# One attention key step in two in split fp32r products, with two output banks and the weight split moved behind the attention

## What is computed

```
mod = silu(c) @ ada_w.T + ada_b                       # shift, scale, gate for attention and for the MLP
qkv = modulate(rmsnorm(x)) @ qkv_w.T + qkv_b           # q and k are rms-normed per head
attn = softmax(q k^T / 6);  o = attn v                 # B=2, H=16, N=2048, 36 wide
x = x + tanh(gate_msa) * (o @ proj_w.T + proj_b)
x = x + tanh(gate_mlp) * (gelu(modulate(rmsnorm(x)) @ fc1_w.T) @ fc2_w.T)
```

## Time and profile before

| what | us |
|---|---|
| median of 3 runs | 3037.22 (3037.14 to 3039.31) |
| the profiled execution | 3036.84, its span 3035.0 |
| TensorE matmuls busy | 2951.3 (97%) |
| ACT busy | 1574.1 (52%) |
| VectorE busy | 1208.0 (40%) |
| POOL busy | 204.6 (7%) |

### The profile page before, as it was taken

How to read it: one execution, slowest core, us unless ns; L and a number is a source line. 1 busy time by engine, 2 the same in 40 slices (tenths; PEclk the granted TensorE clock), 3 DMA queues, 4 the chain that set the end, 5 groups by cost and what they waited for, 6 DMA issues and landing times.

```text
span 3035.0 us, 36177 instructions
## 1 busy us (share of the span) xinstructions
PE 2951.3 (97%) x12968; PEld 1903.2 (63%) x12968; DVE 1208.0 (40%) x1540; ACT 1574.1 (52%) x1918; POOL 204.6 (7%) x126
## 2 busy tenths in 40 slices
PE   7999996999999999999999999999999999999998
PEld 7898993444444444444444444578888888888886
DVE  5887872333322322322322322434242442424242
ACT  3333323666666666666666666644343443434342
POOL 3232303520000000000000000000000000000000
PEclk7999997999999999999999999999999999999999
DMA  5454535232221222222222223131322222232121
GB/s 206 146 190 156 177 131 193 71 100 70 72 78 56 69 79 71 67 75 62 68 74 75 69 68 105 55 102 48 109 88 72 85 73 76 82 104 90 39 70 44
DMA packets 215540, 278.24 MB, mean 92 GB/s; under 512 B 15984, under 2 KB 125040, under 8 KB 214384
## 3 DMA queue, kind: packets, MB, share of 16 engines
q1 hardware_dynamic: 210160, 266.11, 27.7%
q10 hardware_dynamic: 5248, 10.49, 1.0%
HBM read 191.86 MB, written 84.67 MB: 91 GB/s over the span
## 4 chain that ended last, share of the span: by engine, by line
PE 80%; DVE 2%; DMA 1%; ACT 1%; SPq 0%; issue 0%; POOL 0%; DVEq 0%; POOLq 0%
PE ps L1257 23%; PE ps L1246 17%; PE ps L1307 14%; PE ps L1294 14%; PE ps L1256 7%; PE ps L1272 4%; ACT gated L1032 1%; DVE x L1164 0%; DMA vp<-v_scratch 0%; DVE rlb L1109 0%; DMA w_raw<-w 0%; DMA l_scratch<-osb 0%; DVE rlb L1103 0%; DVE w_lo L1158 0%; DVE x L1168 0%; DVE x L1170 0%
## 5 line engine op out<-in xcount | busy, mean ns | idle before, releaser
L985 ACT ACTIVATE prob<-ps 128x1024 f32<-128x1024 f32 x1084 | 979.3, 979 | 509.8 <-PE ps L1246 509.8
L1256 PE MATMUL ps<-prob,vp 128*64 128x512 f32 x2048 | 950.1, 601 | 2.7 <-DMA vp<-v_scratch 1.8
L1257 PE MATMUL ps<-prob,vp 128*37 128x512 f32 x2048 | 942.9, 598 | 0.0
L1246 PE MATMUL ps<-qT,kT 110*128 110x512 f32 x2048 | 564.4, 412 | 20.0 <-DMA qT<-m_scratch 18.7
L1246 PEld LDWEIGHTS ps<-qT,kT 110*128 110x128 f32 x2048 | 360.9, 189 | 346.0 <-ACT prob L985 193.5
L1257 PEld LDWEIGHTS ps<-prob,vp 128*37 128x37 f32 x2048 | 207.3, 114 | 389.2 <-issue 389.2
L1020 ACT ACTIVATE act<-ps,f1b_t 128x512 f32<-128x512 f32 x144 | 99.2, 689 | 509.1 <-PE ps L1294 509.1
L1097 DVE COPY osb<-ps 101x512 f32<-101x512 f32 x64 | 44.3, 692 | 751.8 <-PE ps L1257 748.6
L1256 PEld LDWEIGHTS ps<-prob,vp 128*64 128x64 f32 x2048 | 254.2, 136 | 119.7 <-issue 111.6
L1103 DVE RECIPROCAL rlb<-rlb 101x256 f32<-101x256 f32 x128 | 215.3, 1724 | 253.9 <-DMA rlb<-l_scratch 253.9
L1211 DVE TENSOR_TENSOR a_lo<-act,a_hi 128x512 fp32r<-128x512 f32 x144 | 99.6, 692 | 534.3 <-ACT a_hi L1022 534.3
(11 more groups left out here) (148 smaller groups left out, 2925.6 us busy)
## 6 DMA issues: line engine op xcount, KB each, us to landing
w_raw<-w SPq DMA_DIRECT2D x144, 320.0 KB, 2.9
qk_hi_scratch<-aw SPq DMA_DIRECT2D x32, 576.0 KB, 3.1
qk_lo_scratch<-aw SPq DMA_DIRECT2D x32, 576.0 KB, 4.4
kT<-qk_hi_scratch SPq DMA_DIRECT2D x128, 144.0 KB
qT<-qk_hi_scratch SPq DMA_DIRECT2D x128, 144.0 KB
v_scratch<-stv SPq DMA_DIRECT2D x32, 512.0 KB, 2.6
vp<-v_scratch SPq DMA_DIRECT2D x16, 1024.0 KB, 6.1
xb<-xT SPq DMA_DIRECT2D x8, 1280.0 KB, 9.9
```

The costliest lines, as they stand in the source:

```text
L985: act.activation(prob[:, slot, h0 * BLK:h1 * BLK], src, ACT.Exp).then_inc(exp_done, 1)
L1246: mm = pe.matmul(out, kT[r][:, h, kt * P:(kt + 1) * P], qT[:, c % 2, h], start=True, stop=True)
L1256: pe.matmul(O[0:64], vp[r][:, kt, 0:64], prob[:, j, 0:BLK], start=kt == 0, stop=kt == NT - 1)
L1257: pe.matmul(O[64:VW], vp[r][:, kt, 64:VW], prob[:, j, BLK:2 * BLK], start=kt == 0, stop=kt == NT - 1).then_inc(pv_mm, 1)
```

## The change

Attention is no longer a loop of hardware iterations but written out. The key steps 0 to 3 and 12 to 15 of a unit (SPLITS) are done as "split" steps: DVE makes `p_hi` (a cast, high_p) and `p_lo` (a subtraction, low_p) of the 128x1024 probabilities, and TensorE does four fp32r matmuls, for each head [v_hi | v_lo] (101 columns) times p_hi and times p_lo. Head 0 goes to bank OA and head 1 to bank OBK, where high and low land in partitions 0 to 63 and 64 to 100 (for head 1 the other way round). DVE splits the values once in a group (split_v). The steps 4 to 11 stay fp32 and are done in one block at the unit's end. The values of split steps 12 to 15 are done in the next unit, between its scores 2 and 6.

ACT now empties OBK (take_ob), DVE OA (take_oa); DVE adds the halves (combine: two copies and two additions). The sums are loaded spread over 128 partitions, inverted as 128x8 (invert_sums), stored, and loaded back broadcast; the rest of the unit's ending (finish_o) comes one unit later. The new buffers lie where the split `w2` was, so `w2` is loaded after the last value matmul, in four parts, and split by POOL during MLP block 0. `wp` is split by POOL in five pieces in the early units.

```diff
+RING = 3
+SPLITS = (0, 1, 2, 3, 12, 13, 14, 15)
+EARLY = NS // 2
+HIGHS = 6
...
+    LATE = (OS - W2) // (8 * D)
+    W2_FROM = (0, 2, 8, LATE)
...
         def spread_sums(u):
-                sp.wait_ge(o_evac, u + 1)
+                sp.wait_ge(o_comb, 2 * u + 2)
                 for h in range(2):
+                    sp.dma_start(lt[64 * h:64 * h + 64],
+                                 osb[64 * h + HD:64 * h + HD + 1].rearrange("a (p j) -> a p j", p=64)).then_inc(lt_ld, 16)
+                sp.wait_ge(l_rec, u + 1)
+                sp.dma_start(l_s.rearrange("h (p j) -> (h p) j", p=64), lt[:]).then_inc(l_st, 16)
+                sp.wait_ge(l_st, 16 * u + 16)
+                sp.dma_start(rlb[0:64], l_s[0].partition_broadcast(64)).then_inc(l_ld, 16)
+                sp.dma_start(rlb[64:VW], l_s[1].partition_broadcast(VW - 64)).then_inc(l_ld, 16)
...
+            for u in range(NU):
+                g, c = u // C, u % C
+                if u + 1 < NU:
+                    load_q(u + 1)
...
+                if u == LAST:
+                    sp.wait_ge(s_mm, NT * LAST)
+                    load_x(0)
+                if u > 1:
+                    store(u - 2)
+                if u == LAST:
+                    sp.wait_ge(o_dma, ODMA * (LAST - 2))
+                    load_o(0)
+                if u > 0:
+                    spread_sums(u - 1)
+                if u == LAST + 3:
+                    load_o(1)
+            sp.wait_ge(s_mm, NT * NU)
             load_w1(0)
             load_w1(1)
-            sp.wait_ge(pv_mm, NT * NU)
+            sp.wait_ge(fv_mm, NW * NU)
             load_x(1)
+            sp.wait_ge(rv_mm, NS * NU)
+            load_w2(0, 2)
+            load_w2(2, 8)
+            load_w2(8, LATE)
+            store(NU - 2)
             spread_sums(NU - 1)
-            store(NU - 1, PAIRS - 1, 1, C - 1)
             load_o(2)
...
+            pool.wait_ge(hlo_done, KC)
             for k in range(FC):
+                if k in W2_FROM:
+                    pool.wait_ge(w2_ld[W2_FROM.index(k)], 16)
```

ACT:

```diff
+            for u in range(NU):
+                for kt in range(NT):
+                    if NT * u + kt in PROJ_BEFORE:
+                        proj_gate(0, PROJ_BEFORE.index(NT * u + kt))
+                    if u > 0 and kt == 6:
+                        take_ob(u - 1)
+                    exps(u, kt)
+                if u == LAST + 2:
+                    for m in range(KC):
+                        act.wait_ge(x1_done, m + 1)
+                        act.activation(tmp[:, m], x1[0][:, m], ACT.Square).then_inc(sq_done, 1)
```

DVE (VectorE):

```diff
+            def combine(u):
+                dve.wait_ge(oa_evac, u + 1)
+                dve.wait_ge(ob_evac, u + 1)
                 wait(dve, o_dma, ODMA * u)
...
+            for u in range(NU):
+                if u > 1:
+                    finish_o(u - 2)
+                high_p(u, 0)
+                high_p(u, 1)
+                low_p(u, 0)
+                high_p(u, 2)
+                low_p(u, 1)
+                if u > 0:
+                    take_oa(u - 1)
+                high_p(u, 3)
+                low_p(u, 2)
+                low_p(u, 3)
+                if u > 0:
+                    combine(u - 1)
+                if u % C == 2 and u // C + 1 < NG:
+                    split_v(u // C + 1)
...
+                if u == LAST + 3:
+                    sum_squares(0)
+                high_p(u, 4)
+                high_p(u, 5)
+                low_p(u, 4)
+                high_p(u, 6)
+                low_p(u, 5)
+                if u > 0:
+                    invert_sums(u - 1)
+                high_p(u, 7)
+                low_p(u, 6)
+                low_p(u, 7)
...
+            reciprocal(0, 0)
+            reciprocal(0, 1)
+            finish_o(NU - 2)
+            take_oa(NU - 1)
+            for m in range(KC):
+                normed(0, m)
+            combine(NU - 1)
+            add_proj(1, 0)
+            add_proj(1, 1)
             for m in range(KC):
                 h_low(0, m)
+            invert_sums(NU - 1)
             split_w1(0)
```

TensorE:

```diff
+            for u in range(NU):
+                for kt in range(3):
+                    score(u, kt)
+                for j in range(EARLY):
+                    if u > 0:
+                        split_value(u - 1, EARLY + j)
+                    if j < 3:
+                        score(u, 3 + j)
...
+                for kt in range(6, 9):
+                    score(u, kt)
+                for j in range(EARLY):
+                    split_value(u, j)
+                    if j < 3:
+                        score(u, 9 + j)
...
+                for kt in range(12, NT):
+                    score(u, kt)
+                for kt in WHOLE:
+                    value(u, kt)
+            sum_rows(0)
+            proj(1, 0)
+            for j in range(EARLY, NS):
+                split_value(NU - 1, j)
+            for m in range(1, KC):
                 proj(1, m)
```

More of the change, by code:

```diff
@@ L608, in _, with place, ring_of_step, ring_of_proj @@
                 turn(NTILES - 1, 1)
[L611 to L619, removed]
+RING = 3
 C = NIT
 NU = B * PAIRS * C
+NG = B * PAIRS
 LAST = NU - C
 NB = B * NIT
[L626 to L651, removed]
+SPLITS = (0, 1, 2, 3, 12, 13, 14, 15)
+NS = len(SPLITS)
+EARLY = NS // 2
+WHOLE = range(EARLY, NT - EARLY)
+NW = len(WHOLE)
+HIGHS = 6
+PROJ_BEFORE = (NT * LAST + 12, NT * (LAST + 1) + 6, NT * (LAST + 1) + 12, NT * (LAST + 2) + 6, NT * (LAST + 2) + 12)
+def place(u):
+    return u // C // B, u // C % B, u % C
+def ring_of_step(n):
+    return n + sum(n >= b for b in PROJ_BEFORE)
+def ring_of_proj(m):
+    return PROJ_BEFORE[m] + m
+SUMS_ENTRY = NT * NU + KC
 def columns_of(i):
@@ L704, in main_phase @@
     here[0] = SQ
+    rb0 = at("rb0", [P, BLK], F32, here[0])
     sq0 = following("sq0", [P, 2, BLK], F32R)
@@ L893, in _ @@
             sp.wait_ge(kones, 1)
-            load_k(0, 0, 0)
-            load_q(0, 0, 0, 0)
+            load_k(0, 0)
+            load_q(0)
+            load_v(0)
             for c in range(1, C):
[L897 to L931, removed]
@@ L987, in proj_gate, with take_ob @@
+            def take_ob(u):
+                act.wait_ge(rv_mm, NS * (u + 1))
+                wait(act, o_comb, 2 * u)
+                act.activation(ob[:], OBK[0:VW], ACT.Copy).then_inc(ob_evac, 1)
             def proj_gate(i, m):
@@ L1249, in values, with ring_free @@
-            def values(u, r, kts, final):
-                for kt in kts:
-                    if kt == 0:
-                        wait(pe, o_evac, u)
-                    pe.wait_ge(exp_done, exps_before(u) + exp_index(kt, 1, final) + 1)
-                    j = kt % PSLOTS
-                    pe.matmul(O[0:64], vp[r][:, kt, 0:64], prob[:, j, 0:BLK], start=kt == 0, stop=kt == NT - 1)
-                    pe.matmul(O[64:VW], vp[r][:, kt, 64:VW], prob[:, j, BLK:2 * BLK], start=kt == 0,
-                              stop=kt == NT - 1).then_inc(pv_mm, 1)
+            def ring_free(entry):
+                before = entry - RING
+                for m in range(KC):
+                    if before == ring_of_proj(m):
+                        pe.wait_ge(pgate_done, m + 1)
+                        return
+                wait(pe, exp_done, before + 1 - sum(before > ring_of_proj(m) for m in range(KC)))
@@ new lines, in score @@
+            def score(u, kt):
+                it, r, c = place(u)
+                entry = ring_of_step(NT * u + kt)
+                if kt == 0:
+                    pe.wait_ge(q_ld[u % 2], QDMA * (u // 2 + 1))
+                if c == 0 and kt % TPB == 0:
+                    pe.wait_ge(k_ld[r][kt // TPB], KDMA * (it + 1))
+                ring_free(entry)
+                for h in range(2):
+                    mm = pe.matmul(ps[:, 2 * (entry % RING) + h, :], kT[r][:, h, kt * P:(kt + 1) * P], qT[:, u % 2, h],
+                                   start=True, stop=True)
+                mm.then_inc(s_mm, 1)
```

366 lines of the change are left out of this document (196 added, 170 removed).

## The result

| kernel | median us | range | runs |
|---|---|---|---|
| before | 3037.18 | 3035.46 to 3039.31 | 4 |
| changed | 3350.39 | 3346.11 to 3357.6 | 4 |

The changed kernel takes 1.1033 times as long, with a 95% interval of 1.101 to 1.1056: 313 us more, where I had forecast 3035 us and a range that ended at 3070. Its profiled span is 3351.6 us, against 3035.0.

A forecast was written before the change was run, and what follows sets the result against it. TensorE's own pace was taken to bound the attention, before and after the change. From 3037 us: attention 27 less, start 4 less, last group 5 more, transition to the MLP 24 more, giving 3035 us; range 3006 to 3070.

The forecast's parts named there:

- sums out and back: In each unit, inverted sums stored and loaded back broadcast, from invert_sums to finish_o: 3.8 us.
- the ring: In each attention unit, the loop of waits through DVE, the sums' transfers, TensorE and ACT: 22.1 us, shorter than 22.45.
- score 15's wait: In each unit, TensorE stands 0.57 us before score 15, which needs exponential 12.
- Rival 2: Slower: DVE is the bound in attention, 23.0 us a unit without instruction overlap, 3065 to 3070 us in all; chance 0.20.
- TensorE's work: In each attention unit, matmuls and changes between fp32r and fp32 sum to 21.8 us, about 1.0 below 22.87.
- rival 3: Far slower: in attention every change of stationary shape costs time, 185 us in 64 units, about 3220 us; chance 0.04.
- 0.3 us to spare: In each attention unit, the margin by which the loop of waits through DVE is shorter than TensorE's 22.45 us.
- Attention, 27 us less: Over 64 attention units, 22.45 us each in place of 22.87: 27 us less.
- DVE's durations: In each attention unit, 0.61 us for high_p and 1.13 for low_p with overlap; DVE's work 19.5 of 22.4 us.
- Start, 4 us less: From first matmul to first evacuation, 33 us before: 4 us less, between 0 and 8.
- Last group, 5 more: In the last attention group, 2.5 us waiting for load_o(0) and 2.5 for held-back exponentials: 5 us more.
- Attention to MLP, 24 more: Between attention and fc1, waits for load_o(1) and for the store behind w2: 24 us more, between 14 and 31.

The follow-up runs named there:

- e1: Changed kernel with the second load of the sums to 36 rows instead of 37; 3064.21 us, 1.009 times before.
- e10: Changed kernel with the second load of the sums over 64 rows instead of 37; 3102.29 us, 1.0212 times before.
- e2: Changed kernel, still 37 rows, with the query, key and value loads issued after store(u - 2); 3267.52 us, 1.0761 times before.
- e7: e1 with the waits of the transition to the MLP removed and score 12 issued before split value 3; 3013.79 us, 0.992 times before.
- e8: e7 with load_o(0) one unit earlier and the query, key and value loads issued after store(u - 2); 3005.79 us, 0.9897 times before.
- e4: Changed kernel, still 37 rows, with finish_o(u - 2) moved behind DVE's eight split steps, before combine(u - 1); 3091.88 us, 1.0184 times before.

## Why the prediction was wrong

**The step that failed** is the term "sums out and back" of the ring through DVE: "with one store 3.6, and up to 4.2 if its 128 short rows land slower: 3.8". It measured 8.1. I took its price from two loads of 36 rows; the change issues one of 64 and one of 37, and I held a load of 37 to be a load of 36. The trace has it on one DMA engine instead of 12: 2.7 of the 4.3 us. The loads issued behind it are 1.0. The last 0.6 stay in e1: there the two loads take 1520.83 - 1517.84 = 3.0 us from the first issue, where two of 36 rows took 2.3. I looked for the risk in the short rows on the other side, which cost nothing. With the way put in, the ring comes near the units of all the runs:

| kernel | way of the sums | ring: 22.1 - 3.8 + way | unit measured |
|---|---|---|---|
| e1 | 4.4 | 22.7 | 22.68 |
| e10 | 4.9 to 5.4 | 23.2 to 23.7 | 23.37 |
| e2 | 7.1 | 25.4, and slow matmuls after some pauses | 26.1 |
| changed | 8.1 | 26.4, and 1.5 of slow matmuls: 27.9 | 27.7 |

In e10, e2 and the changed kernel TensorE waits for take_oa in every unit, so there the ring does set the pace. In e1 the agreement is in part luck: by the trace TensorE waits for take_oa in 16 of 41 units only, 0.12 us in the mean, and its own work with score 15's wait is the other 22.5. So the ring of my sum is 0.2 us too long.

The 1.5 us I had nowhere: where a ring has TensorE stand for 3.5 us in each trip, its restart at half clock is part of the trip. Rival 2 named the right mechanism, "DVE is the bound", with the idle time of TensorE released by take_oa as its mark; at 0.4 us for the sums' way it was a tenth of the true size.

The other steps are best read in e1, where that term is nearly gone:

- **TensorE's work** of 21.8 us: e7's and e8's best units take 21.95 to 22.0. The split values start 0.233 apart, not 0.228, which is 0.16 of it. No drain shows between scores and split values; rival 3 is out.
- **Score 15's wait** is there, and shorter: 0.21 us of idle time, 0.37 by the distance of starts, for the 0.57. Moving score 12 took 0.42 us off the stretch from split value 0 to the fp32 block, but TensorE's wait for take_oa rose from 0.12 to 0.26 us a unit, so that 0.27 came off the unit. e1's unit is 22.68 and not 22.45 by these 0.12 of the ring and 0.1 of TensorE's own. My 0.3 us to spare were not there in every unit: with 36 rows the way is 4.4 and up to 6.1, not 3.8.
- **Attention, 27 us less**: over the first 59 units it is 4 us less (22.80 for 22.87; units 3 to 12, with the weight split of POOL beside them, take up to 24.1; that POOL is the reason was not tried).
- **DVE's durations** (high_p 0.683, low_p 1.219, every 0.60 and 1.14) and the overlap were right. By the rule on the quadrants of 32 partitions (the Trainium skill, VectorE: DVE Perf Modes, the section on two Vector instructions with no wait between them), the trace agrees: what starts at partition 0 overlaps.
- **Start, 4 us less**: 2.7 (30.4 us to the first evacuation in place of 33.0; 32.1 in the changed kernel).
- **Last group, 5 more**: 6.0 (three units take 91.7 in place of 85.6), where the sum had 5 - 3 x 0.42 = 3.7.
- **Attention to MLP, 24 more**: 27. proj(1, 0) waits for load_o(1), and combine for the store that is behind w2, each as the prediction has it. The waits in e1, 1880:2025:

```profile
DVE rlb L1143 <- DMA o_lo_scratch<-osb: 11.8, 1, 11.8
PE ps L1393 <- DMA o_hi<-o_lo_scratch: 11.3, 1, 11.3
```

  fc1 starts 46.5 us after the last fp32 block, where I had 43.4; in the changed kernel it is 46.5 too.

With 36 rows the kernel is 28 us slower than before, 3064 for 3036; my sum had 2 less than before. Of these 30 us the unit is 21 (60 x 0.35), the transition 3, the MLP 2.4 (1041.9 from fc1 to the end, before 1039.5), the last group 2 and the start 1.

## What to carry to other kernels

Before a transfer on a chain of waits is priced by a row of the trace, its number of rows has to be that of the row: 36 and 37 rows are 3.6 us apart here, and one that isn't read can be left out or split off. When work is moved to an idle engine, the first instruction in its queue that waits for a transfer sets the pace of all that is behind it; putting it behind the unit's first eight steps (e4) took back 258 us without touching the transfer. A ring with 0.3 us to spare in the mean binds in some of its trips (16 of 41 in e1): count every term at its upper end and see what the next bound is.

## What the runs showed that I had not expected

- A load of 37 rows of 2 KB lands 6.1 us after its issue with other loads behind it, about 5.2 without (e2: issued at 1508.92, used at 1514.09); one of 36 rows 2.5, one of 36 and one of 1 together 2.3, one of 64 rows 2.8 to 3.5. (Means of units 17 to 58: 5.9, 4.9, 2.4, 2.4, 3.1.)
- By its updates of the semaphore a load of 37 rows goes through one DMA engine, one of 36 through 12; its rows follow each other every 0.08 us (e2).
- The same loads behind it cost 1.0 us to the transfer of 37 rows and nothing that shows to the one of 36.
- After a pause of 3.5 us TensorE's granted clock is 0.50, and its matmuls 0.43 us apart. At 1.5 us a unit that is an estimate of 64 x 1.5 = 96 us, a third of the whole loss (109 with the mean of 1.7), and no engine shows it as idle time.
